# Scores of two head pairs grouped in the batch loop of a gated cross-attention layer, with their maxima read beside other products

## The reference

```python
x = x + jnp.tanh(g_xattn[0]) * _L0_xattn_ref(_layernorm(x, axis=-1), ctx_1024, ctx_1024, mask_BxS2_bf0, ...)
x = x + jnp.tanh(g_ffn[0]) * _L0_ffn_ref(_layernorm(x, axis=-1), ...)

# _L0_xattn_ref
q = (queries @ Wq + bq).reshape(b, sq, H, DK).transpose(0, 2, 1, 3)
k = (keys @ Wk + bk).reshape(b, sk, H, DK).transpose(0, 2, 1, 3)
v = (values @ Wv + bv).reshape(b, sk, H, DV).transpose(0, 2, 1, 3)
scores = jnp.einsum('bhqd,bhkd->bhqk', q, k) / jnp.sqrt(jnp.float32(DK))
scores = jnp.where(mask[:, None, None, :], NEG_INF, scores)
scores = jnp.where(causal[None, None], NEG_INF, scores)
attn = jax.nn.softmax(scores, axis=-1)
out = jnp.einsum('bhqk,bhkd->bhqd', attn, v)
return out @ Wo + bo

# _L0_ffn_ref: the expert of the largest routing logit
indices = jnp.argmax(jax.nn.softmax((x @ Wr + br) / TEMPERATURE, axis=-1), axis=-1)
for i in range(num_experts):
    xi = x * (indices == i).astype(x.dtype)[..., None]
    out = out + (jax.nn.relu(xi @ W1[i] + b1[i]) @ W2[i] + b2[i])
```

## Time and profile before

| | us |
|---|---|
| median of 3 runs | 360.89 (360.82 to 364.35) |
| the profiled execution | 365.85 |
| its span, first to last instruction | 363.8 |
| mean granted clock of TensorE | 0.998 |
| loop of batches 1 to 6, in the span | 60.63 to 273.50 |

### The profile page before, as it was taken

One profiled execution on the slowest core, in us unless ns is written; L12 is line 12 of the kernel. 1 busy time (PEld: TensorE's weight loads), 2 busy tenths in 40 slices (PEclk: granted clock), 3 DMA queues, 4 the chain that ended last, 5 costly groups with the idle time before them and its releaser, 6 DMA issues.

```text
span 363.8 us, 11160 instructions
## 1 busy us (share of the span) xinstructions
PE 345.6 (95%) x2835; PEld 283.3 (78%) x2835; DVE 270.9 (74%) x1262; ACT 255.5 (70%) x936; POOL 191.0 (52%) x369
## 2 busy tenths in 40 slices
PE   8999999999999999999999999999999897978893
PEld 6776778778878787878778877887887666968893
DVE  4789995878687868786878687867777696776671
ACT  3686775887687868785878587859773667646562
POOL 7245555366537744774467436833681570345544
PEclk9999999999999999999999999999999999999999
DMA  6999202000400030004000400040005914133320
GB/s 201 248 367 244 91 2 90 4 2 1 122 0 0 0 119 0 0 0 119 0 0 0 119 0 0 17 117 0 0 29 211 366 36 133 50 104 105 89 66 13
DMA packets 21562, 27.87 MB, mean 77 GB/s; under 512 B 3649, under 2 KB 16789, under 8 KB 21536
## 3 DMA queue, kind: packets, MB, share of 16 engines
q1 hardware_dynamic: 19776, 23.85, 21.7%
q0 software_dynamic: 1504, 3.16, 2.5%
q10 hardware_dynamic: 256, 0.56, 0.5%
HBM read 19.00 MB, written 9.01 MB: 77 GB/s over the span
## 4 chain that ended last, share of the span: by engine, by line
PE 80%; DVE 10%; issue 3%; ACT 3%; DVEq 1%; DMA 1%; another core or an unknown queue 1%; POOLq 0%; SPq 0%; POOL 0%; ACTq 0%
PE ps_kv L1255 15%; PE ps_o L1255 13%; PE ps_s L1255 13%; PE ps_t L1359 11%; PE ps_w L1255 10%; PE ps_q L1255 8%; PE ps_t L1255 7%; DVE masked L823 2%; DVE prob_T L842 2%; PE ps_s L1479 1%; ACT prob L565 1%; PE ps_w L1396 1%; DMA nat<-in_ctx 1%; DVE row_fix L830 1%
## 5 line engine op out<-in xcount | busy, mean ns | idle before, releaser
L433 POOL TENSOR_SCALAR prob<-prob,row_inv 128x128 f32<-128x128 f32 (+1 forms) x256 | 104.8, 429 | 124.9 <-DVE row_inv L836 124.7
L565 ACT ACTIVATE prob<-masked,neg_max 128x128 f32<-128x128 f32 (+1 forms) x256 | 113.7, 447 | 65.5 <-DVE neg_max L823 65.2
L823 DVE CUSTOM_DVE_ANT_0 masked<-ps_s,mask_now 128x128 f32<-128x128 f32 (+1 forms) x256 | 77.8, 353 | 44.3 <-PE ps_s L1255 40.8
L842 DVE COPY prob_T<-ps_t 128x384 f32<-128x384 f32 x123 | 65.0, 549 | 0.8 <-PE ps_t L1359 0.7
L1255 PE MATMUL ps_s<-k_T,q_T 64*128 64x128 f32 (+1 forms) x512 | 59.6, 351 | 1.5 <-DVE neg_max L823 1.5
L1359 PEld LDWEIGHTS ps_t<-ident,prob 128*128 128x128 f32 x384 | 41.0, 141 | 21.5 <-issue 17.3
L1359 PE MATMUL ps_t<-ident,prob 128*128 128x128 f32 x384 | 56.1, 282 | 0.6 <-DVE prob_T L842 0.5
L1255 PE MATMUL ps_o<-prob_T,v_nat 128*64 128x256 f32 (+1 forms) x512 | 49.8, 333 | 2.1 <-DVE prob_T L842 1.5
L565 ACT ACTIVATION_READ_ACCUMULATOR prob<-masked,neg_max 128x1 f32 x256 | 48.5, 190 | 0.0
L1255 PEld LDWEIGHTS ps_o<-prob_T,v_nat 128*64 128x64 f32 x512 | 31.7, 136 | 16.3 <-issue 2.1
L1255 PEld LDWEIGHTS ps_s<-k_T,q_T 64*128 64x128 f32 x512 | 33.9, 188 | 9.7 <-issue 6.8
(11 more groups left out here) (200 smaller groups left out, 545.9 us busy)
## 6 DMA issues: line engine op xcount, KB each, us to landing
ctx_buf<-in_ctx SPq DMA_DIRECT2D x8, 768.0 KB
sorted_rows<-pad_rows SPq DMA_DIRECT2D x8, 642.5 KB, 4.4
tile_in<-sorted_rows SPq DMA_DIRECT2D x24, 128.5 KB, 2.1
packs<-in_L_ffn_W SPq DMA_DIRECT2D x1, 2048.0 KB
packs<-in_L_ffn_W SPq DMA_DIRECT2D x8, 256.0 KB
nat<-in_ctx SPq DMA_DIRECT2D x8, 128.0 KB, 3.4
nat<-in_x SPq DMA_DIRECT2D x1, 768.0 KB, 6.6
w_in<-in_L_xattn_Wk SPq DMA_DIRECT2D x2, 256.0 KB, 4.5
```

The source lines that it names most:

```text
L433: g.tensor_scalar(prob[:, slot, lo:hi], prob[:, slot, lo:hi], row_inv[:, slot, t:t + 1], 1.0, ALU.mult, ALU.mult).then_inc(prob_ready, 1)
L565: s.activation(prob[:, slot, lo:hi], masked[:, slot % 2, lo:hi], ACT.Exp, bias=neg_max[:, slot, t:t + 1], scale=-1.0, accum_out=row_sum[:, ...
L823: v.tensor_tensor_reduce(out=masked[:, slot % 2, lo:hi], in0=ps_s[slot % 2][:, lo:hi], in1=mask_now[:, lo:hi], scale=-SCALE, scalar=FLOOR, ...
L842: v.tensor_copy(prob_T[:, slot % TSLOTS, :], ps_t[slot % 2][:, 0:W3]).then_inc(probT_kept, 1)
```

## The change

Only the loop of batches 1 to 6 gets a new body, `loop_batch`, in four groups g of two pairs; batches 0 and 7 are adapted to it at their seam. In a group PE does the transposes of pair p, one query projection and its keys and values, the second query projection, the transposes of pair p + 1, the second keys and values, the values products of both pairs, and then the scores of two pairs at once (`two_scores`). The scores of the second pair's second query tile go to halves of the banks `ps_kv` and `ps_q`; therefore the next group's first projection waits for the first of the `shared_maxima`, which DVE takes first, and its keys and values for the second. The last group's scores stand directly ahead of the output projection. The tile `masked` goes: the masked scores are written to `prob`, and the exponentials are computed in place. DVE takes over every second copy of a query projection (`keep_q`). The input transposes move to bank `ps_w`. The small steps move: the second norm to groups 0 and 1, the choice to 2 and 3, the ranks behind the last keys and values, the placing behind them, the residual ahead of the last group's products on POOL, and the scatter between these. In batch 7 the norm of batch 6 is spread wider.

```diff
--- before.py
+++ after.py
...
+def a_pair(g):
+
+    return (2 * g + PAIRS - 2) % PAIRS
...
-        masked = sb("masked", [P, 2, W3])
...
+        ps_s2 = [ps_kv[:, 0:S], ps_q[:, S:2 * S]]
...
+            def loop_batch(b):
+                for g in range(PAIRS // 2):
+                    if g == 2:
+                        sum_context(b + 1)
+                    if g == 3:
+                        residual_of(b)
+                    for i in range(SUMS, SUMS + 2):
+                        for h in range(2):
+                            normalise(8 * b + 2 * g + i, h, (2 * (2 * g + i) + h) % SLOTS)
+                        if g == 3 and i == SUMS:
+                            scatter(b - 1)
...
-                s.activation(in_T[:, :], ps_q[:, :], ACT.Copy).then_inc(inT_ready, 1)
+                s.activation(in_T[:, :], ps_w[:, :], ACT.Copy).then_inc(inT_ready, 1)
...
-                    s.activation(prob[:, slot, lo:hi], masked[:, slot % 2, lo:hi], ACT.Exp,
+                    s.activation(prob[:, slot, lo:hi], prob[:, slot, lo:hi], ACT.Exp,
                                  bias=neg_max[:, slot, t:t + 1], scale=-1.0,
                                  accum_out=row_sum[:, slot, t:t + 1]).then_inc(exp_done, 1)
...
+            def two_exponentials(p, j, which, heads=(0, 1)):
+
+                for h in heads:
+                    exponential(p + which, h, (2 * (j + which) + h) % SLOTS,
+                                4 * p + (7 + h if which else 4 + 2 * h))
...
+            def loop_batch(b):
+                for g in range(PAIRS // 2):
+                    j, p = 2 * g, 8 * b + 2 * g
+                    a = 8 * b + PAIRS - 2 + j
+                    if g == 0:
+                        context_now(b + 1)
+                    if g == 2:
+                        keep_y(b)
+                    if g == 0:
+                        two_exponentials(p + SUMS, j + SUMS, 0)
+                        two_exponentials(p + SUMS, j + SUMS, 1, (0,))
+                    keep_q(a, a_pair(g))
+                    keep_kv(a, a_pair(g))
+                    if g == 1:
+                        keep_mean(b)
+                    if g == 2:
+                        keep_x2T(b - 1)
+                    if g > 0:
+                        two_exponentials(p + SUMS, j + SUMS, 0)
+                    else:
+                        two_exponentials(p + SUMS, j + SUMS, 1, (1,))
+                    keep_kv(a + 1, a_pair(g) + 1)
+                    if g > 0:
+                        two_exponentials(p + SUMS, j + SUMS, 1)
+                    if g == 0:
+                        keep_inT(b + 1)
+                    for i in range(2):
+                        keep_oT(b, p + i, j + i, p + 2)
...
+            def masked_maximum(slot, t, scores):
+
+                lo, hi = ((0, P), (P, W3))[t]
+                v.tensor_tensor_reduce(out=prob[:, slot, lo:hi], in0=scores, in1=mask_now[:, lo:hi], scale=-SCALE,
+                                       scalar=FLOOR, op0=ALU.add, op1=ALU.min,
+                                       accum_out=neg_max[:, slot, t:t + 1]).then_inc(max_ready, 1)
...
-                    v.tensor_tensor_reduce(out=masked[:, slot % 2, lo:hi], in0=ps_s[slot % 2][:, lo:hi],
-                                           in1=mask_now[:, lo:hi], scale=-SCALE, scalar=FLOOR, op0=ALU.add,
-                                           op1=ALU.min, accum_out=neg_max[:, slot, t:t + 1]).then_inc(max_ready, 1)
+                    masked_maximum(slot, t, ps_s[slot % 2][:, lo:hi])
+
+            def shared_maxima(p, j):
+
+                dve.wait_ge(scores_done, p + 2)
+                dve.wait_ge(probT_done, 2 * (p + 2) - SLOTS)
+                settle(dve)
+                for h in (1, 0):
+                    masked_maximum((2 * j + 2 + h) % SLOTS, 1, ps_s2[h])
+
+            def own_maxima(j, h):
+
+                for t, (lo, hi) in enumerate(((0, P), (P, W3))):
+                    masked_maximum((2 * j + h) % SLOTS, t, ps_s[h][:, lo:hi])
+
+            def short_maxima(j):
+
+                for h in range(2):
+                    masked_maximum((2 * j + 2 + h) % SLOTS, 0, ps_s[h][:, W3:W3 + P])
...
+            def keep_q(p, j):
+
+                dve.wait_ge(q_done, p + 1)
+                v.tensor_scalar(q_T[:, j, :], ps_q[:, 0:S], bias_T[:, j:j + 1], None, ALU.add).then_inc(q_dve, 1)
...
+            def loop_batch(b):
+                for g in range(PAIRS // 2):
+                    j, p = 2 * g, 8 * b + 2 * g
+                    shared_maxima(p + SUMS, j + SUMS)
+                    if g > 0:
+                        for h in range(2):
+                            keep_probT(p, h, (2 * j + h) % SLOTS)
+                    for h in range(2):
+                        own_maxima(j + SUMS, h)
+                    if g == 3:
+                        for step in (3, 4, 5):
+                            choose(b - 1, step)
+                    short_maxima(j + SUMS)
+                    if g == 0:
+                        normalise_x(b + 1)
+                        for h in range(2):
+                            keep_probT(p, h, (2 * j + h) % SLOTS)
+                    for h in range(2):
+                        keep_probT(p + 1, h, (2 * j + 2 + h) % SLOTS)
+                    keep_q(8 * b + PAIRS - 1 + j, a_pair(g) + 1)
+                    if g == 3:
+                        for step in range(4):
+                            place(b - 1, step)
+                    fix_sums(p + SUMS, 2 * (j + SUMS) % SLOTS)
+                    invert_sums(p + SUMS, 2 * (j + SUMS) % SLOTS)
+                    for step in ((0, 1, 2, 3, 4), (5, 6, 7, 8, 9, 10, 11), (), ())[g]:
+                        second_norm(b - 1, step)
+                    if g == 2:
+                        for step in range(3):
+                            choose(b - 1, step)
+                        dve.wait_ge(max_ready, 4 * 8 * (b + 1))
+                        mask_of(b + 1)
+                    if g == 3:
+                        sum_context(b + 1)
+                    fix_sums(p + AHEAD, 2 * (j + AHEAD) % SLOTS)
+                    invert_sums(p + AHEAD, 2 * (j + AHEAD) % SLOTS)
...
-                all_q_kept(b - 1)
+                if isinstance(b, int) and b == 1:
+                    all_q_kept(0)
+                else:
+                    pe.wait_ge(x2_ready, 2 * (b - 1))
                 for t in range(QT):
-                    t_.transpose(ps_q[:, t * P:(t + 1) * P], x_norm[:, t, :], ident[:, :])
+                    t_.transpose(ps_w[:, t * P:(t + 1) * P], x_norm[:, t, :], ident[:, :])
                 for t in range(QT):
-                    last = t_.transpose(ps_q[:, S + t * P:S + (t + 1) * P], ctx_now[:, t, :], ident[:, :])
+                    last = t_.transpose(ps_w[:, S + t * P:S + (t + 1) * P], ctx_now[:, t, :], ident[:, :])
                 last.then_inc(inT_done, 1)
...
+            def two_scores(p, j, b, nb, nj):
+
+                pe.wait_ge(k_kept, p + 2)
+                for i in range(2):
+                    q_kept(b, j + i)
+                pe.wait_ge(max_ready, 4 * p)
+                for i, lo in ((0, 0), (1, W3)):
+                    for h in range(2):
+                        score(ps_s[h][:, lo:lo + P], j + i, h, 0)
+                for h in range(2):
+                    score(ps_s[h][:, P:W3], j, h, 1)
+                pe.wait_ge(k_kept, p + 4)
+                pe.wait_ge(v_kept, p + 4)
+                q_kept(nb, nj)
+                for h in range(2):
+                    score(ps_s2[h], j + 1, h, 1).then_inc(scores_done, 1)
...
+                    pe.wait_ge(q_act, PAIRS // 2 * b)
+                    pe.wait_ge(q_dve, PAIRS // 2 * b)
...
+                if last:
+                    for h in range(2):
+                        transpose_probs(8 * b, h, h)
+                    pe.wait_ge(max_ready, 4 * (8 * b + SUMS) + 1)
+                    project_q(b, PAIRS - 2)
+                    pe.wait_ge(max_ready, 4 * (8 * b + SUMS) + 2)
+                    project_kv(b, PAIRS - 2)
...
                     tile_transpose(0, 0)
                     last_projection(PAIRS - 1)
                 else:
+                    two_scores(8 * (b + 1) + SUMS, SUMS, b + 1, b + 1, PAIRS - SUMS - 1)
...
+            def loop_batch(b):
+                for g in range(PAIRS // 2):
+                    j, p = 2 * g, 8 * b + 2 * g
+                    nb, a = (b, PAIRS - 2) if g == 0 else (b + 1, j - 2)
+                    for h in range(2):
+                        transpose_probs(p, h, (2 * j + h) % SLOTS)
+                    if g == 2:
+                        mean_through_wvo(b)
+                    pe.wait_ge(max_ready, 4 * (p + SUMS) + 1)
+                    project_q(nb, a)
+                    pe.wait_ge(max_ready, 4 * (p + SUMS) + 2)
+                    project_kv(nb, a)
+                    if g == 1:
+                        mean_of(b)
+                    if g == 2:
+                        norm_transposes(b - 1, b + 1)
```

(26 more changed lines are left out.)

106 lines of the change are left out of this document (53 added, 53 removed).

## The result

The changed kernel takes 359.44 us, the median of 10 runs (359.04 to 363.07), against 362.59 for 10 runs of the kernel before (360.82 to 364.35): the ratio is 0.9937, 95% interval 0.9914 to 0.996, so some 2.3 us or 0.6% faster (the medians lie 3.15 apart). I had forecast 355.0, 1.6% faster. The profiled execution took 359.95, its span is 358.2 at a granted clock of 0.994.

A forecast was written before the change was run, and what follows sets the result against it. PE was taken as the bound, busy 212.72 of 212.87 us. Per batch -1.85 + 0.5 + 0.3 + 0.15 = -0.9; six batches -5.4 and seams -0.5 gave -5.9, from 360.89 to 355.0 us, range 350 to 361.5.

The forecast's parts named there:

- The saving on PE: Per loop batch on PE, fewer losses at changes of the array's shape: 3.85 before, 2.00 after, 1.85 us saved.
- grouping saves nothing inside: Rival, chance 0.07: in scores groups the second pair costs 0.85, saving 1.05 a batch instead of 1.85; 359.8 us.
- the walk of the seams: Between the loop's groups, PE's new waits for DVE and ACT: 0.5, 0.3 and nothing, plus 0.15 smaller terms a batch.
- small terms: Across a loop batch, restarts after waits (0.05 each) and last values perhaps waiting for copies (0.1): 0.15 us in the sum.
- Group 1, "nothing added": Group 0 to group 1, PE behind the input transposes: no added wait, up to 0.3 us if ACT is late again.
- the copy's 0.86: Input copy behind group 1's input transposes: needs 0.20 + 0.61 + 0.05 = 0.86 us before PE can project.
- Group 2, "wait 0.5": Ahead of group 2's first query projection: PE ready at 7.46, let go by DVE's first shared maximum at 8.0; wait 0.5 us.
- my 0.20: Time assumed for each hand-over between engines in the walks: 0.20 us, with bounds 0.05 and 0.44.
- Group 3, "wait 0.3": Ahead of group 3's first query projection: PE ready at 7.68, let go by DVE at 7.9 to 8.0; wait 0.3 us.
- The seams outside the loop: At batches 0 and 7, one scores group of two replaces one of each: 0.15 + 0.35 = 0.5 us saved.
- DVE and ACT take over: Rival, chance 0.16: their cycle sets groups 1 and 2, waits of 0.95 and 0.75 eat the gain; 360.9 us.
- The signs: Expected in the changed profile: scores 1.5, batch 34.6, PE waits before groups 2 and 3, DVE idle behind scores under 10 us.

The follow-up runs named there:

- a break: Full-array product of 128 columns inside each scores group, against the changed kernel with input copy halved and norm and choice steps moved earlier: 368.25 us.
- The split copy: Changed kernel with ACT's copy of the transposed inputs cut in two, the first query projection waiting for the first piece alone: 359.51 us.
- the shorter norm: Changed kernel whose loop leaves out two of the three refinement rounds of the second norm: 358.15 us.

## Why the prediction was wrong

- **The saving on PE** was right. I took 1.85 a batch. A batch of the changed kernel less its 2.19 of losses is 35.52 - 2.19 = 33.33, one of the kernel before less its 0.26 is 35.45 - 0.26 = 35.19: 1.86 less. The second pair of scores costs the bare 0.65 (1.51 for both), and a break costs 0.36 to 0.40 where I had 0.35. The rival that grouping saves nothing inside is out.
- **The failed step is the walk of the seams**: 0.5 ahead of group 2, 0.3 ahead of group 3, nothing at group 1 and 0.15 for small terms, 0.95 in all, where 1.93 were added (2.19 found, of which the kernel before had 0.26). That turns the 0.9 a batch that I forecast into 0.07 more. Its parts:
  - Group 1, "nothing added": 0.45, of which the kernel before had 0.21 at the same place. I called the copy's 0.86 covered since PE had waited there before, too. But only 0.66 stand between now, so 0.2 were missing by my own numbers. And the copy starts at 138.57 and takes 0.60, but PE starts 0.24 behind its end, where I had 0.05 from the trace before: 1.04 were needed. The split copy returned 0.22.
  - Group 2, "wait 0.5": 0.67 + 0.18. The chain was the right one, as the shorter norm shows. Two of its hand-overs are shorter than my 0.20 (the last exponential's sum is out at 143.64 and DVE starts at 143.67; the maximum is over at 147.58 and PE starts at 147.64), but the norm took 2.76 us (143.98 to 146.74) instead of the 2.27 of the earlier trace rows, where POOL did nothing beside it; the last section shows what held it. The 0.18 are the two slow starts.
  - Group 3, "wait 0.3" plus 0.1 for the last values: 0.80. Only 0.13 of it is the wait that I walked. 0.42 is in the values, which I gave 0.1 without walking DVE: choice, short maxima, copies of the second transposes. Moving three steps of the choice returned it whole. The rest is the slow starts.
- **The seams outside the loop**: I took 0.5. Batch 7 gave 1.87, of which 1.16 is the spread norm, an edit that I named in no term at all. It is half of the 2.3 us that the ratio shows.
- **The rival "DVE and ACT take over"** gave 360.9 with waits of 0.95, 0.75 and 0.15 a batch (its sum leaves out the 0.5 of the seams; with it, it is 360.4). The mechanism is the one measured, in other places and a little larger, and the measured total lies between it and my forecast only because batch 7 gained. Its sentence from the Trainium skill (TensorEngine Tiling (Array Packing), Performance Considerations), that the evacuation of PSUM can become the bottleneck, fits the waits, most of which end with a reader of PSUM. But not as a limit of capacity: with nearly the same instructions in another order the period is 34.27.
- **Batch 0** is 1.1 shorter in the profile; the later kernels, alike there, spread over 1.7 (55.26 to 56.94), so this is no finding.
- **The signs.** Scores of 1.51 in a row, PE waiting for maxima ahead of groups 2 and 3 and not in group 0, and DVE's idle time behind scores at 3.9 came as written; the batch of 34.6 did not (35.52).
- **Luck.** From the profiled execution of before my sum gave 359.95, and the profiled execution of the changed kernel took exactly that. The parts don't agree: the loop was 0.5 longer instead of 5.4 shorter, and the 5.9 come from batch 7 (1.9), from the stretches ahead of the loop and behind batch 7 (1.1 and 3.1), which moved by 1.7 and 2.6 between executions of kernels alike there, and from 0.3 outside the span; the 0.5 of the loop goes off.

## What to carry to other kernels

When a change takes away PE's own losses, price it by the walk of every queue that then becomes late, and walk the group from its first to its last instruction: the place that I didn't walk (copies behind the choice) cost as much as the one that I did. An engine with idle time in total can still be late in every group; look for where it waits early and move the small steps there, which here, with the input copy in halves, was worth 1.25 us a batch for no saved work, and the same steps two lines too late cost 1.4. Ask also what a moved step's own wait will meet: the norm's first step met the scatter in five batches of six until the scatter, too, was earlier. Read a diff's small table entries as edits of their own: one changed line of batch 7's norm brought half of the measured gain.

## What the runs showed of the hardware

DVE's small steps on data in SBUF took up to twice as long beside POOL's products. The norm's half steps, two of one column each, took 0.35 for the pair alone and 0.57 at 144.64, while POOL did this:

```profile
144.23 1.63 POOL L438 TENSOR_SCALAR prob<-prob,row_inv 128x128 f32<-128x128 f32 x4 [4.52 <-DVE row_inv L916]
```

In the single records of the changed kernel's trace, 21 such half steps lie beside POOL's tensor operations for at least 95% of their length; 13 of them took 0.41 to 0.43 us and 8 took 0.21 to 0.24. Of 25 beside none, none took over 0.22. Each of the 13 ends within 0.01 us of the end of one of POOL's products, and 12 of them began 0.07 behind that product's start: the step is held until the product is over. In the traces of the runs above, too, every half step of over 0.3 us ends with a product of POOL. Two such steps, and the one at 144.33 ahead of them (0.27 instead of 0.16), account for the 0.49 by which the norm of group 1 exceeded its price.

DVE's copies of the probabilities from PSUM don't show it: 0.552 (52 of them) against 0.547 (50). Why the one kind is held and the other not was not tried.
